# Moving a DMA broadcast from GpSimd's queue to the SP queue, with the stage orders chosen anew

## The chip, the core and the metric

The kernel runs on one core of a Trainium2 chip. The metric is the device time of one execution in microseconds (us). Engines are called as in the profile: PE (TensorE's matmuls), DVE (VectorE), ACT (ScalarE), POOL (GpSimd) and SP (SyncE, which here only issues DMAs).

## What is computed

The reference is a two-layer transformer block over 16 batch items of 256 tokens by 256 features, in float32. Cut to what matters here:

```python
xn = layernorm(x)                          # layer 0, per batch item
x  = x + attention0(xn) + gated_ffn(xn)    # 16 heads, hidden size 704
xn = layernorm(x)                          # layer 1
scores  = sigmoid(xn @ gate_w)             # 32 experts
combine = top-6 of scores, divided by their sum, zero elsewhere     # [token, expert]
g, u    = xn @ wg[e], xn @ wu[e]           # 96 hidden features for each expert e
routed  = sum over e of combine[:, e] * ((silu(g) * u) @ wd[e])
shared  = (silu(xn @ sg) * (xn @ su)) @ sd # 192 hidden features
x  = x + attention1(xn) + routed + shared
```

All 32 experts are computed for every token, and the routing weight multiplies the hidden activations.

## The kernel before

**Streams and bodies.** Batch items go through a software pipeline. One loop body (13 of them, iterations 2 to 14 of the 16 items; prologue and epilogue are written out with their own orders) works on four items at once, in five streams: stream 0 is layer 0 of one item (its queries `q0..q15`, the ffn chunks, the keys `k0..k15`), stream 1 is layer 1 of the item before (`o1`, `op`, `ln2`, `x`, `gram`, `k`, `rs+v`, `router`, `comb`, the stack loads, `Q0..Q14`, `MAX`, `K0..K14`, `T1`, `O`), streams 2 and 3 are the experts (stream 3 units 0 to 6 of that same item, stream 2 units 7 to 13 of the item before it), and stream 4 is the front of the next item (`f.ln`, `f.x`, `f.q`, `f.k`, `f.v`, `f.land`). These short names are used below and in the prediction.

**What sets the order.** Every engine runs the same list of stages, `ORDERS[...]`, a string of digits written out by hand: each digit names the stream whose next stage comes. Each engine is in order, so an instruction that waits for a semaphore holds everything behind it on that engine, and on SP a waiting DMA holds every later DMA.

**An expert unit** covers 256 hidden rows (two chunks of 128; units 0 and 1 are the shared expert and smaller). `gate` n: PE makes g in the bank s3r0 (12 matmuls), ACT takes tanh (L907), DVE makes `gs` (L1210), POOL multiplies it by the broadcast routing weights `cb2` (L704). `up` n: PE makes u in s3r1, DVE multiplies it by that product (L1205), ACT rounds it to half precision (L903), POOL makes the low part `h2l` (L713). `down` n: PE multiplies both by `wd` into s2acc (L1321).

**The routing weights.** Layer 1's router leaves [expert, token] weights in `comb_d` in DRAM (L511). `broadcast(group)` (L681 to L686) copies the weights of three units onto the 128 partitions of half of `cb2` with six DMAs, so four groups, 24 DMAs and 3 MB, for each item. Groups 0 and 1 are issued in stage `weights`, group 2 once POOL has finished the product of unit 4, and group 3 once it has finished that of unit 7, which frees their halves.

**The chain through SP.** When PE has made the values of the next item (`f.v`), ACT copies them to `v1`, and SP stores them (L458), loads the query and key rows (`land1`, 12 DMAs, L466), which DVE copies into `qst1` and `kst1` (L1027, stage `st`, needed by `q0`), then stores layer 0's attention output with 16 DMAs (L494), turns into the next body, and loads it back as `ot1` (L501, printed as xn<-o_d), which PE turns in stage `o1` (L1330, printed as s2r<-ident,xn).

Of the kernel before, what the change touches and what calls it, by code (L numbers as in the profile page):

```python
# [65 lines left out]
def prev(it):  # L66

    if isinstance(it, int):
# [12 lines left out]
    "body": ("022002102112020100102102212122210220210020121101212211131003201023100101011011310030004031"  # L81
             "40300040303043003433030330341333301"),
    "start": ("102003121002200012202302110030001030000221333131033100130000110020014121042110210033401132"
             "02341100012021310032304243131223121"),
    "first": ("010011220102012200010131011202030003020013211031201111010011321102112211310000400310422320"
             "32020240320043004013303103342323303"),
    "late": ("402220012014022102104101022121222102220120010021210121211413120301003102101331013311013303"
             "00140000330030034030000010303033133"),
    "end": ("220402100214201220121120121202400212200201222012140111011013312202113110313000030103011033"
             "03104030330143003000000133010303303"),  # L90
# [3 lines left out]
def program(nc, a, out):  # L94
# [22 lines left out]
    with ctx:  # L117
# [11 lines left out]
        def sem(name):  # L129
            if name not in sems:  # L130
                sems[name] = ctx.enter_context(nc.semaphore(name))
            return sems[name]
# [97 lines left out]
        cb2 = sb("cb2", [P, PAIRS, S])  # L230
# [303 lines left out]
        def sp3(sp, it, part):  # L534
            for kind, n in part:
                if (kind, n) == ("gate", 0):
                    sp.wait_ge(*emptied2(it, U2["x"]))
                    if prev(it) is not None:
                        sp.wait_ge(*event("ring3_full1", it, 0))
                    sp.dma_start(xe[:, :, :, :].rearrange("p g k s -> p (g k s)"),  # L540
                                 part2[:, 0:2, :, :].rearrange("p g k s -> p (g k s)")).then_inc(sem("xe_loaded"), 16)
                if kind == "out":
                    sp.wait_ge(*event("acc2_free", it, 1))
                    carry(sp, "sp_waited")
                    sp.dma_start(one(out, it).rearrange("b (t p) e -> p (b t) e", p=P), xbe[:, :, :]).then_inc(sem("out_saved"), 16)
                if (kind, n) != part[-1]:
                    yield
# [130 lines left out]
        def gp3(gp, it, part):  # L678
            g = nc.gpsimd

            def broadcast(group):  # L681
                src = one(comb_d, it).rearrange("b (a f) s -> f (b a) s", f=4)
                for i, first, count, which in ((0, 0, 3, 0), (0, 3, 1, 1), (1, 0, 2, 1), (1, 2, 2, 2), (2, 0, 1, 2), (2, 1, 3, 3)):
                    dst = cb2[32 * first:32 * (first + count), 6 * (group % 2):6 * (group % 2) + 6, :].rearrange("p (a i) s -> p a i s", i=3)[:, :, i, :]
                    gp.dma_start(dst, src[which, 2 * group:2 * group + 2].partition_broadcast(32 * count)  # L685
                                 ).then_inc(sem(f"cb2_loaded{group % 2}"), 16)  # L686

            for kind, n in part:
# [4 lines left out]
                if kind == "weights":  # L693
                    gp.wait_ge(*event("gc2_made", it, 0))
                    gp.wait_ge(*event("comb_saved", it, 16))
                    carry(gp, "gp_waited")
                    broadcast(0)
                    broadcast(1)
                if kind == "gate" and n >= 2:
# [6 lines left out]
                    if p in (2, 5):  # L706
                        gp.wait_ge(*event("gc2_made", it, p + 1))
                        broadcast(p // 3 + 2)
# [1019 lines left out]
```

## Time and profile before

| | |
|---|---|
| median of three runs | 2131.82 us (2128.59 to 2132.87) |
| the profiled execution, its own time | 2133.93 us |
| its span, first to last instruction | 2132.2 us |
| mean granted clock of PE | 0.968 of full speed |
| instructions | 48392 |
| period of the loop body, mean of twelve between two stores of the output | 124.4 us (1820.82 - 328.36 over 12) |

The profiled execution lies within 0.1% of the median, and its span is 1.7 us shorter than its own time. The first 268 us are set-up and prologue, the loop ends near 1885 us, and the last 80 us hold one item's rest, mostly its expert units alone.

### The profile page before, as it was taken

The numbers are of one execution on the slowest core, as the hardware profiler recorded it, in microseconds if no ns is written. First come the engines' busy times: TensorE is split into PE (matmuls) and PEld (weight loads), VectorE is DVE, ScalarE is ACT, GpSimd is POOL, SyncE is SP. The second block draws the span as 40 slices with busy tenths as digits, with TensorE's granted clock in tenths as the row PEclk, the third lists the DMA queues.
The fourth block names the chain that finished last, engine by engine and source line by source line (L and its number), as shares of the span: only waits on it lengthen the run. The fifth ranks groups of instructions, "written<-read, shape, count | busy, mean of one in ns | idle before, by whom it ended". The sixth has DMA issues, their size and how long they took to land.

```text
span 2132.2 us, 48392 instructions
## 1 busy us (share of the span) xinstructions
PE 1774.9 (83%) x16112; PEld 1340.1 (63%) x16112; DVE 1117.8 (52%) x2564; ACT 828.9 (39%) x1598; POOL 855.4 (40%) x988
## 2 busy tenths in 40 slices
PE   2747888889888888988888888888889888888887
PEld 1424666757666675766667576675757667676766
DVE  3566373655637365563636556373655637365442
ACT  2352425343343534334253433535343343533432
POOL 2003343534344353434435343443535344354445
PEclk7678999999999999999999999999999999999999
DMA  5452322313132132313213131321313132232111
GB/s 114 93 146 63 56 54 59 74 49 81 39 85 54 58 67 58 78 39 85 54 57 74 51 80 39 85 55 52 73 52 84 39 85 55 58 70 56 47 60 35
DMA packets 323775, 139.28 MB, mean 65 GB/s; under 512 B 228048, under 2 KB 309008, under 8 KB 323600
## 3 DMA queue, kind: packets, MB, share of 16 engines
q1 hardware_dynamic: 305168, 86.24, 17.9%
q0 software_dynamic: 18432, 50.36, 8.8%
q8 instruction: 153, 2.51, 0.5%
q14 instruction: 22, 0.18, 0.0%
HBM read 102.12 MB, written 29.88 MB: 62 GB/s over the span
## 4 chain that ended last, share of the span: by engine, by line
issue 33%; PE 28%; POOL 11%; DVE 11%; ACT 7%; SPq 6%; DMA 3%; POOLq 0%; ACTq 0%; DVEq 0%
PE s3r L1324 8%; POOL gs L704 4%; PE s2acc L1321 4%; POOL h2l L713 3%; SPq L494 2%; POOL cb L685 2%; PE s2r L1324 2%; SPq L519 2%; PE s1acc L1427 1%; ACT p L872 1%; PE s2r L1532 1%; ACT p L812 1%; DVE th L1205 1%; PE s2r L1575 1%; PE s1a L1324 1%
## 5 line engine op out<-in xcount | busy, mean ns | idle before, releaser
L704 POOL TENSOR_TENSOR gs<-gs,cb 128x512 f32<-128x512 f32 x192 | 243.8, 1270 | 403.0 <-DVE gs L1210 401.6
L713 POOL TENSOR_TENSOR h2l<-th,h2h 128x512 f16<-128x512 f32 (+1 forms) x224 | 247.1, 1103 | 355.6 <-ACT h2h L903 353.3
L903 ACT CAST h2h<-th 128x512 f16<-128x512 f32 (+1 forms) x224 | 131.7, 588 | 538.0 <-DVE th L1205 485.2
L1324 PE MATMUL s3r<-xe,xg 128*128 128x256 f16 x2304 | 285.7, 274 | 20.8 <-issue 20.8
L1321 PE MATMUL s2acc<-xd,h2h 128*128 128x256 f16 x1536 | 270.4, 278 | 19.3 <-POOL h2l L713 19.3
L1324 PE MATMUL s3r<-xe,xu 128*128 128x256 f16 x2304 | 283.3, 273 | 0.2 <-DVE th L1205 0.2
L1210 DVE SCALAR_TENSOR_TENSOR gs<-th,s3r 128x512 f32<-128x512 f32 (+1 forms) x224 | 144.9, 647 | 240.2 <-ACT th L907 240.0
L1324 PEld LDWEIGHTS s3r<-xe,xg 128*128 128x128 f16 x2304 | 223.9, 98 | 54.6 <-issue 25.0
L685 POOL DMA_DIRECT2D cb<-comb_d x384 | 229.6, 604 | 35.9 <-POOL gs L704 20.1
L1324 PEld LDWEIGHTS s3r<-xe,xu 128*128 128x128 f16 x2304 | 225.3, 98 | 27.3 <-DVE th L1205 0.5
L907 ACT ACTIVATE th<-s3r 128x512 f32<-128x512 f32 (+1 forms) x224 | 126.5, 565 | 274.0 <-PE s3r L1324 270.5
L1205 DVE TENSOR_TENSOR th<-s3r,gs 128x512 f32<-128x512 f32 x192 | 132.5, 690 | 164.4 <-POOL gs L704 152.8
L1321 PE MATMUL s2acc<-xd,h2l 128*128 128x256 f16 x768 | 213.6, 278 | 0.0
L1321 PEld LDWEIGHTS s2acc<-xd,h2h 128*128 128x128 f16 x1536 | 149.5, 99 | 50.4 <-POOL h2l L713 25.3
L650 POOL TENSOR_TENSOR h1p<-th,h1p 128x256 f16<-128x256 f32 x96 | 64.5, 671 | 235.2 <-ACT h1p L800 166.0
L1160 DVE TENSOR_REDUCE m<-s2r 128x3 f32<-128x384 f32 x256 | 131.0, 552 | 38.2 <-PE s2r L1534 33.3
L872 ACT ACTIVATE p<-s2r 128x384 f32<-128x384 f32 x256 | 111.1, 485 | 59.1 <-PE s2r L1578 59.1
L1532 PE MATMUL s2r<-stacks 126*128 126x128 f16 (+1 forms) x512 | 85.8, 256 | 45.5 <-DMA stacks<-part_d 28.7
L1038 DVE TENSOR_REDUCE mx<-s1a 128x2 f32<-128x512 f32 x128 | 87.6, 684 | 17.5 <-PE s1a L1403 16.3
L1532 PEld LDWEIGHTS s2r<-stacks 126*128 126x128 f16 x512 | 38.9, 100 | 90.1 <-DVE m L1160 51.0
L1038 DVE TENSOR_REDUCE mx<-s1b 128x2 f32<-128x512 f32 x128 | 87.5, 684 | 10.6 <-PE s1b L1403 10.5
L1575 PE MATMUL s2r<-stacks 128*128 128x256 f16 (+1 forms) x512 | 73.9, 249 | 19.2 <-DMA stacks<-mt 6.1
(279 smaller groups left out, 3125.9 us busy)
## 6 DMA issues: line engine op xcount, KB each, us to landing
cb<-comb_d POOLq DMA_DIRECT2D x128, 192.0 KB, 3.4
part_d<-part SPq DMA_DIRECT2D x32, 512.0 KB, 3.2
cb<-comb_d POOLq DMA_DIRECT2D x128, 128.0 KB, 3.1
stacks<-part_d SPq DMA_DIRECT2D x192, 64.0 KB, 2.3
va<-v_d SPq DMA_DIRECT2D x512, 8.0 KB
cb<-comb_d POOLq DMA_DIRECT2D x128, 64.0 KB, 3.1
land<-part_d SPq DMA_DIRECT2D x96, 64.0 KB, 2.5
part<-part_d SPq DMA_DIRECT2D x96, 64.0 KB, 4.2
```

The lines of the kernel that those rows point to most:

```text
L685: gp.dma_start(dst, src[which, 2 * group:2 * group + 2].partition_broadcast(32 * count)).then_inc(sem(f"cb2_loaded{group % 2}"), 16)
L704: g.tensor_tensor(gc2[:, p % 2, :], gs2[:, p % 2, :], cb2[:, 2 * (p % 6):2 * (p % 6) + 2, :].rearrange("p a s -> p (a s)"), ALU.mult).then ...
L713: g.tensor_tensor(h2l[0:m, n % 2, 0:w], th2[0:m, n % 2, 0:w], h2h[0:m, n % 2, 0:w], ALU.subtract).then_inc(sem("h2l_made"), 1)
L872: s.activation(p2[:, i % PSLOT, :], ring2[u % 2][:, 0:3 * P], ACT.Exp, scale=L ** -0.5).then_inc(empties2(u), 1)
L903: s.copy(h2h[0:m, n % 2, 0:w], th2[0:m, n % 2, 0:w]).then_inc(sem("h2h_made"), 1)
L1038: v.tensor_reduce(mx1[:, h, :], two(bk), AX.X, ALU.max).then_inc(empties1(u), 1)
L1160: v.tensor_reduce(m32[:, h, :], bk[:, 0:3 * P].rearrange("p (c n) -> p c n", n=P), AX.X, ALU.max).then_inc(empties2(u), 1)
L1205: ins = v.tensor_tensor(th2[0:m, s, 0:w], bk[0:m, 0:w], gc2[0:m, s, 0:w], ALU.mult)
L1210: v.scalar_tensor_tensor(gs2[0:m, s, 0:w], th2[0:m, s, 0:w], 1.0, ring3[0][0:m, 0:w], ALU.add, ALU.mult).then_inc(empties3(0), 1)
L1321: ins = nc.tensor.matmul(bk, lhs[i][k], rhs[j][k], start=first and chain[0], stop=last and chain[1], skip_group_check=True)
L1324: ins = nc.tensor.matmul(bk, lhs[i][k], rhs[j][k], start=first, stop=last)
L1532: mm(bk[:, P * j:P * j + P * (j + 1)], query(qst2, h, OPEN)[:, P * j:P * j + P], key(kst2, h, OPEN)[:, 0:P * (j + 1)], start=j == 0, stop= ...
```

## The change

The six-DMA helper `broadcast` moves from the GpSimd program `gp3` to the SP program `sp3`, with the same sources, destinations and semaphores. Groups 2 and 3 were issued by POOL behind its own product of unit 4 and 7, in the stages `gate4` and `gate7`; SP now waits for the semaphore of that product (`gc2_made`) in the same stages. All five order strings are replaced, for every engine.

```diff
 ORDERS = {
-    "body": ("022002102112020100102102212122210220210020121101212211131003201023100101011011310030004031"
-             "40300040303043003433030330341333301"),
+    "body": ("222020210011002210101220121022210212022200121002121111103123031321003100130101301101000401"
+             "03401300040304330030033040343301333"),
...
         def sp3(sp, it, part):
+            def broadcast(group):
+                src = one(comb_d, it).rearrange("b (a f) s -> f (b a) s", f=4)
+                for i, first, count, which in ((0, 0, 3, 0), (0, 3, 1, 1), (1, 0, 2, 1), (1, 2, 2, 2), (2, 0, 1, 2), (2, 1, 3, 3)):
+                    dst = cb2[32 * first:32 * (first + count), 6 * (group % 2):6 * (group % 2) + 6, :].rearrange("p (a i) s -> p a i s", i=3)[:, :, i, :]
+                    sp.dma_start(dst, src[which, 2 * group:2 * group + 2].partition_broadcast(32 * count)
+                                 ).then_inc(sem(f"cb2_loaded{group % 2}"), 16)
...
+                if kind == "weights":
+                    sp.wait_ge(*event("gc2_made", it, 0))
+                    carry(sp, "sp_waited")
+                    sp.wait_ge(*event("comb_saved", it, 16))
+                    broadcast(0)
+                    broadcast(1)
+                if kind == "gate" and n in (4, 7):
+                    sp.wait_ge(*event("gc2_made", it, n - 1))
+                    broadcast((n - 4) // 3 + 2)
...
         def gp3(gp, it, part):
...
-                if kind == "weights":
-                    gp.wait_ge(*event("gc2_made", it, 0))
-                    gp.wait_ge(*event("comb_saved", it, 16))
-                    carry(gp, "gp_waited")
-                    broadcast(0)
-                    broadcast(1)
...
-                    if p in (2, 5):
-                        gp.wait_ge(*event("gc2_made", it, p + 1))
-                        broadcast(p // 3 + 2)
```

Read as stages, the end of one body and the start of the next, up to `o1`, hold these after `f.v`. Before: down2 gate4 k15 up4 weigh3 down3 gate5 turned1 up5 f.land O down4 gate6 up6 down5 outproj, then st gate7 up7 q0 q1 down6 o1. Now: turned1 gate5 f.land up5 down4 outproj gate6 up6 down5, then gate7 up7 down6 st gate8 q0 up8 o1.

On the SP queue the start of the loop body stood like this before (`va` are the loads of layer 0's values, `xn<-o_d` the load for `o1`):

```order
L477 DMA va<-v_d 8x16x16
L477 ISA
L477 DMA va<-v_d 8x16x16
L477 ISA
L477 DMA va<-v_d 8x16x16
L477 ISA
L477 DMA va<-v_d 8x16x16
L497 REGISTER_ALU
L500 ISA
L501 ISA
L501 DMA xn<-o_d 128x2x256
```

and now:

```order
L539 DMA cb<-comb_d 96x2x256
L539 ISA
L539 DMA cb<-comb_d 32x2x256
L539 DMA cb<-comb_d 64x2x256
...
L477 DMA va<-v_d 8x16x16
L477 ISA
L477 DMA va<-v_d 8x16x16
L497 REGISTER_ALU
L500 ISA
L501 ISA
L501 DMA xn<-o_d 128x2x256
```

Six broadcasts of group 3 (three of them in the rows left out) now stand ahead of the load for `o1`, and two value loads in place of four.

On DVE the start of the loop body before:

```order
L1306 ISA
L1027 COPY qst<-land 48x8x64 x4
L1027 COPY kst<-part 48x8x64 x4
L1208 ISA
L1209 ISA
L1210 SCALAR_TENSOR_TENSOR gs<-th,s3r 128x512
L1204 REGISTER_ALU
L1205 TENSOR_TENSOR th<-s3r,gs 128x512
L1036 ISA
L1038 TENSOR_REDUCE mx<-s1a 128x2
```

and now:

```order
L1306 ISA
L1209 ISA
L1210 SCALAR_TENSOR_TENSOR gs<-th,s3r 128x512
L1204 REGISTER_ALU
L1205 TENSOR_TENSOR th<-s3r,gs 128x512
L1021 ISA
L1027 COPY qst<-land 48x8x64 x4
L1027 COPY kst<-part 48x8x64 x4
L1208 REGISTER_ALU
L1209 REGISTER_ALU
L1210 SCALAR_TENSOR_TENSOR gs<-th,s3r 128x512
L1036 ISA
```

The copies into `qst` and `kst` now stand behind both halves of unit 7 and ahead of unit 8's `gs`.

On ACT the tanh of unit 9 (L907) now stands between the square root of `ln2` (L762) and that of the key norm (L842). Before:

```order
L762 ACT_TABLE_LOAD
L762 ACTIVATE mv<-mv 128x2
L902 REGISTER_ALU
L903 CAST h2h<-th 128x512
L839 CAST part<-s2r 128x512
L842 ACTIVATE rt<-rt 128x32
```

and now:

```order
L762 ACT_TABLE_LOAD
L762 ACTIVATE mv<-mv 128x2
L907 ACT_TABLE_LOAD
L907 ACTIVATE th<-s3r 128x512
...
L839 CAST part<-s2r 128x512
L842 ACT_TABLE_LOAD
L842 ACTIVATE rt<-rt 128x32
```

The body has six table loads on ACT now, where it had four.

## Rows read from the trace of the kernel before

**Rows 1.** the page: busy share of each engine, with instructions.

```profile
PE 1774.9 (83%) x16112; PEld 1340.1 (63%) x16112; DVE 1117.8 (52%) x2564; ACT 828.9 (39%) x1598; POOL 855.4 (40%) x988
```

**Rows 2.** windows of one body: us; busy PE, PEld, DVE, ACT, POOL; clock, DMA share, GB/s.

```profile
369.66:393.76 24.10, 21.64 (x203) 18.34 (x201) 10.43 (x23) 6.71 (x12) 13.47 (x14) 1.00 0.55 103
393.76:431.67 37.91, 31.70 (x297) 26.40 (x296) 28.26 (x65) 14.51 (x28) 19.36 (x22) 1.00 0.23 60
431.67:492.92 61.25, 53.74 (x507) 37.40 (x508) 28.09 (x69) 28.35 (x57) 19.95 (x25) 1.00 0.16 50
```

**Rows 3.** TensorE's waits in twelve bodies (total us, times, longest).

```profile
PE s2r L1532 <- DMA stacks<-part_d: 24.7, 12, 2.4
PE s2r L1522 <- DVE cm L1152: 23.0, 12, 1.9
PE s3r L1324 <- issue: 20.8, 12, 2.1
...
PE s2acc L1321 <- POOL h2l L713: 9.5, 12, 2.1
...
PE s2r L1330 <- DMA xn<-o_d: 6.4, 7, 2.1
```

**Rows 4.** timeline of the SP queue around the end of a body.

```profile
370.99 0.38 SPq L458 DMA_DIRECT2D v_d<-xn  x1
371.69 2.90 SPq L466 DMA_DIRECT2D land<-part_d  x6
374.77 3.68 SPq L466 DMA_DIRECT2D part<-part_d  x6
379.99 7.70 SPq L494 DMA_DIRECT2D o_d<-th  x16
388.46 1.70 SPq L477 DMA_DIRECT2D va<-v_d  x4
390.61 0.39 SPq L501 DMA_DIRECT2D xn<-o_d  x1
```

**Rows 5.** timeline of TensorE in the same stretch.

```profile
369.44 0.38 PE L1324 MATMUL s1b<-wqkv,x1l 128*128 128x256 f16 x2
...
393.76 0.60 PE L1330 MATMUL s2r<-ident,xn 128*128 128x128 f32 x4
```

**Rows 6.** timeline of all engines, unit 4 from gate matmuls to up product.

```profile
370.96 1.47 PE L1324 MATMUL s3r<-xe,xg 128*128 128x256 f16 x12
...
372.27 0.38 PE L1444 MATMUL s1a<-qst,kst 128*128 128x256 f16 x2
...
372.60 1.47 PE L1324 MATMUL s3r<-xe,xu 128*128 128x256 f16 x12
...
373.87 1.28 POOL L704 TENSOR_TENSOR gs<-gs,cb 128x512 f32<-128x512 f32 x1 [2.28 <-DVE gs L1210]
...
374.00 1.06 PE L1427 MATMUL s1acc<-p,va 128*17 128x256 f32 x16
...
375.18 0.69 DVE L1205 TENSOR_TENSOR th<-s3r,gs 128x512 f32<-128x512 f32 x1 [1.39 <-POOL gs L704]
```

**Rows 7.** instructions by source line: ns min/median/max, first and last start.

```profile
L477 SPq DMA_DIRECT2D va<-v_d x512: 275/278/2792, 51.7 to 1944.9; - x171
...
L558 SPq DMA_DIRECT2D sd_row<-in_L_ffn_s_down x1: 588/588/588, 28.5 to 28.5; - x1
...
L1027 DVE COPY kst<-part x64: 410/420/426, 54.4 to 1885.8; 48x512 f32<-48x512 f32 x64
```

**Rows 8.** timeline of GpSimd, then of TensorE, in the last 80 us.

```profile
2096.59 2.37 POOL L685 DMA_DIRECT2D cb<-comb_d  x4 [1.09 <-issue]
...
2100.20 0.61 PE L1321 MATMUL s2acc<-xd,h2h 128*128 128x256 f16 x2 [3.37 <-POOL h2l L713]
```

**Rows 9.** timeline of ScalarE around the second layer's square roots.

```profile
407.10 1.28 ACT L845 ACT_TABLE_LOAD   x1
408.40 0.22 ACT L845 ACTIVATE el<-s2r 128x64 f32<-128x64 f32 x1
```

More of the change, by code:

```diff
@@ L80 @@
 ORDERS = {
-    "body": ("022002102112020100102102212122210220210020121101212211131003201023100101011011310030004031"
-             "40300040303043003433030330341333301"),
[L83 to L90, printed above, removed]
+    "body": ("222020210011002210101220121022210212022200121002121111103123031321003100130101301101000401"
+             "03401300040304330030033040343301333"),
+    "start": ("103112303000102300212023203012121030330020300101002100130002033000431211310342001112020413"
+             "10022400303100021321111122130114422"),
+    "first": ("001002110011001031101132223000021101021021312302300021210100112111131120001003023243104302"
+             "30301420030304000244230022323310332"),
+    "late": ("220202102410102021002110221012221021220202112121211101310030310221003103031014013110100033"
+             "03400330401003030000434103030333013"),
+    "end": ("022402040240002200201021212011102112021201022202100110112000124410021031002020331100330131"
+             "30013313040000101331331333330133010"),
 }
@@ L679, in gp3 @@
             g = nc.gpsimd
[L681 to L686, printed above, removed]
             for kind, n in part:
```

## The prediction

> **What bounds the kernel now.** The page comes first: PE is busy for 83% of the span, no other engine for more than 52%, POOL for 40% [rows 1]. The page's slices are alike from the eighth on, since the loop runs 13 like bodies, so I cut one body by windows at three joints of PE's order: from the end of `f.v` to `o1` (24.10 us, PE busy 21.64), from `o1` to `Q0` (37.91, busy 31.70), and from `Q0` to the end of the next `f.v` (61.25, busy 53.74) [rows 2]. Together 123.26 us with 107.08 busy: 16.2 us of PE's idleness is all that a new order can win or add to in a body. The chain of waits says who holds PE there. In twelve bodies the layer 1 chain leads: 24.7 us for the stack loads, 23.0 for the router's `cm`, 20.8 for the turn of the loop (`issue`), against 9.5 for POOL's `h2l` and 6.4 for the load that `o1` needs [rows 3]. So POOL, which the change relieves, holds PE for 0.8 us in a body, and SP's chain, which the change loads, for 0.5 us, on average: it is covered, but only just.
>
> That chain is the one to read closely. `f.v` ends on PE at 369.66 (its last two matmuls start at 369.44 and take 0.11 each to the next start) [rows 5]. SP stores the values at 370.99, loads 12 row sets from 371.69, stores layer 0's output with 16 DMAs from 379.99, turns into the next body, loads four value sets, and issues the load for `o1` at 390.61 [rows 4]. PE starts `o1` at 393.76 [rows 5], and no wait is put down there in this body, so 3.15 us was enough for the load to land. SP is nearly without pause from 371.69 to 390.61. PE's own work in that stretch is as long as SP's chain, and that is why neither waits.
>
> **The change part by part.**
>
> *POOL's issues go.* Where they held PE, that stops. In the loop they do so inside the stretch from `f.v` to `o1`, whose length another chain sets below, so I count nothing for it there. In the last 80 us the experts run alone, and the broadcast of group 3 (its last four DMAs take 2.37 us) precedes the `h2l` for which PE waits 3.37 us; PE then runs slower, a pair of matmuls takes 0.61 us [rows 8] where such a pair takes 0.38 [rows 5], as at the lower clock level. I take 3.4 us, 1.7 us for the lower clock (an estimate: half of a stretch as long as the gap), and 0.5 us of shorter waits: 5.6 us gained. Bounds: 3 and 9 us.
>
> *Less PE work covers SP's chain.* Count the stages that the change section lists. Gone from between `f.v` and `o1` are down2, gate4, up4 and down3 (1.31 us each, as gate4 from 370.96 to 372.27), k15 and q1 (0.33 each, 372.27 to 372.60), weigh3 (1.0, from 374.00) [rows 6] and O (0.4, four transposes like those of `o1`); new are gate8 and up8. Net -5.24 - 2.06 + 2.62 = -4.7 us. So PE has 21.64 - 4.7 = 16.9 us to do there, and 107.08 - 16.9 = 90.1 us in the rest of the body.
>
> *The chain itself is no shorter.* From `f.v` to the store 1.33 us, from there to the load for `o1` 19.62 us, from there to `o1` 3.15 us. Off: the gap ahead of the output stores (378.45 to 379.99, of which 0.2 us is ordinary), since `turned1` is now directly behind `f.v` and the stores come later than its result: -1.3; two value loads fewer, of four in 1.70 us with their register instructions: -0.96. On: six broadcasts of group 3. No such DMA from SP is in the trace. Its bounds: a value load's 0.28 us of issue plus 0.1 us around it, and the only partition broadcast timed, `sd_row` at 0.59 plus 0.07 [rows 7]: six take 2.3 to 4.0 us. I take 0.46 us each, near the bulk of SP's DMAs, 2.75 us. The six are free to go: POOL's product of unit 7 comes first. Sum: 24.10 - 1.3 - 0.96 + 2.75 = 24.6 us, bounds 24.1 to 25.9, against 16.9 us of work and 1.7 us for the turn of the loop (20.8 us in twelve [rows 3]). PE waits some 6 us more than nothing here, where it waited 0.5.
>
> Broadcast group 2 stands between the stores of `part_d` and of the values. PE has up3, down2, k12 with its weighing, k13 and gate4 (5.6 us) and then k14, k15, up4, down3, weigh3 and f.v (5.6 us) after `f.k`; POOL's product of unit 4 ends 2.9 us behind its gate matmuls (372.27 to 375.15 [rows 6]), so SP is through about 1 us before the values are there. Hidden; if it is not, each us late is added.
>
> *A second chain in the same place.* DVE's copies for `q0` stand behind unit 7 now. From the end of gate7's matmuls to the end of the up product is 3.6 us (372.27 to 375.8 [rows 6]), eight copies follow, at 0.38 us apart (0.42 each, overlapping) 3.1 us [rows 7]. PE has up7, down6 and gate8 to cover that, 3.9 us: `q0` waits 2.7 us. Were SP's chain instant, `o1` would come 20.9 us after `f.v`. This wait lies under the longer chain and costs nothing more, but it is the floor.
>
> *The rest of the body.* From `o1` on, the same links with other cover, each by its before-wait and by what moved: `op` has lost gate8 as cover, +0.8; `x` to `gram` +1.1; `rs` -0.4; the router's `cm` has ffn0 as new cover, -1.1; the stack loads the same (down11 is new cover, but ACT's copy `ct` stands behind a later tanh); five pairs Q6 to Q14 in a row, which DVE reduces at 1.0 us a pair, +0.6; the K pairs are spaced better, -0.9; `f.x` +0.4. Sum +0.5, bounds -5 and +4, since eight guesses of half a microsecond each can lean one way. In `x` to `gram` 0.7 us comes from ACT: the tanh of unit 9 between two square roots makes two more table loads in a body. One takes 1.28 us here and the activation starts 0.02 us behind it (407.10, 408.40) [rows 9]. The Trainium skill (ScalarE: Activation LUTs, What ACT_TABLE_LOAD costs) adds a drain of about 1.38 us to each switch of tables. By that the body would be up to 1.4 us longer; the trace shows no such drain, so I leave it out.
>
> *Sum.* Body: 24.6 + 90.1 + 13.7 (idle in the two other stretches, 6.21 + 7.51) + 0.5 = 128.9 us against 123.3, +5.6 us. Twelve joints of body to body: +67 us. The last 80 us: -5.6 us. The prologue's and epilogue's orders I count at 0, +-8. Against the profiled execution's own 2133.9 us this gives 2195; that execution is 2 us above the median, so 2193 us.
>
> **The rivals.**
>
> *Refilled cover, faster (0.15).* The work that left the stretch (4.7 us) could be worth more elsewhere: if it falls just into the waits for `cm`, for the stacks and for the K pairs (1.9 + 2.0 + some 3 us a body), the idleness in the rest drops from 13.7 to 7 us. The body is then 24.6 + 90.1 + 7 = 121.7 us, -1.6, so 2131.8 - 19 - 5.6 = 2107 us. It decides from 9.0 us of idleness downwards. For it: nothing but those waits is large. Against: stack loads, `cm` and K pairs keep nearly the cover they had, as counted.
>
> *Half refilled (0.20).* With 11 us of idleness there: 125.7, +2.4, 2155 us; in its lower tail lies no change (0.04).
>
> *Transfers queue on SP's queue, worse (0.15).* The load for `o1` is now issued 1 us behind six broadcasts that write 768 KB; if it lands only behind them, 2 to 3 us later, the body is +8.6 and the time 2229 us. Against: the queue's DMAs finished in about 3 us at the joint even with 16 output stores ahead.
>
> *The issuer does not matter, no change.* The Trainium skill (DMA: Bandwidth & Descriptors, Issuing engines are not separate DMA queues) says that DMAs of all issuers share the same 16 DMA engines, and that another issuer saves only its issue time, usually small. By that, moving them is worth 24 issues a body on either side and the time would be about 2130 us, within the 0.04. The trace agrees that bytes are not the limit (DMA share 0.55 at most [rows 2]), but here issue time lies on a chain, so I give it no more.
>
> **How the numbers follow.** The forecast, 2165 to 2215, has 0.46; with worse 0.15 and the half refilled case's slower part 0.20 this is 0.81 for slower by over 0.2% (what this measurement can tell from no change), 0.04 for the same, 0.15 for faster. The range 2120 to 2240 us leaves out most of the faster rival and the tail of the worse one. The predicted time is the likeliest case's, 2193 us; its own range is 2165 to 2215.
>
> **What would show it.** PE's wait for the load of `o1` rises from 6.4 us in all to 25 us or more, with a wait for the copies into `kst` or `qst` of 2 to 3 us ahead of `q0` in each body, new in the list of waits. From `f.v` to `o1` stays near 24.6 us while PE is busy for about 17 of them; the period of the bodies rises from 124.4 to about 129 us. On SP, six broadcasts at the body's start take 2.3 to 4 us. POOL has 384 instructions fewer, and PE's wait of 3.4 us for `h2l` in the last 80 us is gone. I am wrong if the idleness from `o1` to the next `f.v` falls below 9 us.

## The result: 4.65% slower, and the profile after

The changed kernel takes 2230.35 us (median; 2227.28 to 2235.62), the kernel before 2132.35 us beside it: a ratio of 1.0465, 95% interval 1.0437 to 1.0492. The profiled execution of the changed kernel has a span of 2225.6 us.

The page, busy share of each engine (answers to [rows 1]):

```profile
PE 1819.6 (82%) x16112; PEld 1362.2 (61%) x16112; DVE 1105.2 (50%) x2564; ACT 866.1 (39%) x1624; POOL 625.2 (28%) x604
```

POOL is relieved of 384 instructions and 230 us, and nothing is faster for it. PE, with the same 16112 matmuls, is busy 45 us longer: a part of it ran at a lower granted clock.

Windows of one body, cut at the same three joints as [rows 2]: from the end of `f.v` to `o1`, to `Q0`, to the end of the next `f.v`:

```profile
645.07:672.30 27.23, 18.21 (x152) 15.05 (x150) 10.97 (x22) 5.09 (x9) 9.90 (x8) 0.94 0.47 108
672.30:710.15 37.85, 32.80 (x286) 26.59 (x285) 24.41 (x60) 15.67 (x27) 12.67 (x13) 0.91 0.15 39
710.15:776.97 66.82, 60.13 (x572) 42.23 (x570) 30.62 (x73) 31.77 (x64) 15.73 (x16) 1.00 0.17 51
```

The first window holds 152 matmuls in place of 203 and is 3.1 us longer; PE is idle in it for 9.0 us, where it was idle for 2.5. In the two others it is idle for 11.7 us, where it was for 13.7. The clock is 0.94 and 0.91 in the first two; it was 1.00 in all three.

PE's waits between 300 and 1900 us, which hold twelve bodies (answers to [rows 3]; total us, times, longest):

```profile
PE s2r L1330 <- DMA xn<-o_d: 43.8, 12, 6.3
PE s1a L1401 <- DVE kst L1027: 38.5, 12, 3.7
PE s3r L1324 <- issue: 25.9, 12, 2.6
...
PE s2r L1532 <- DMA stacks<-part_d: 15.1, 13, 1.4
...
PE s2r L1522 <- DVE cm L1152: 8.8, 13, 0.7
```

The load for `o1`, next to nothing before (6.4), leads, and the copies into `kst` are new. The waits for the stacks and `cm` have shrunk by 24 us together.

Timeline of SP's queue around the same joint (answers to [rows 4]):

```profile
641.96 4.09 SPq L539 DMA_DIRECT2D cb<-comb_d  x6
646.28 0.42 SPq L458 DMA_DIRECT2D v_d<-xn  x1
647.01 2.92 SPq L466 DMA_DIRECT2D land<-part_d  x6
650.11 3.10 SPq L466 DMA_DIRECT2D part<-part_d  x6
653.40 6.60 SPq L494 DMA_DIRECT2D o_d<-th  x16
663.22 3.70 SPq L539 DMA_DIRECT2D cb<-comb_d  x6
667.61 0.75 SPq L477 DMA_DIRECT2D va<-v_d  x2
668.81 0.40 SPq L501 DMA_DIRECT2D xn<-o_d  x1
```

The six broadcasts before the load take 3.70 us. Ahead of them is a hole: the last store is issued at 660.00, the first broadcast at 663.22, and nothing is waited for. That is SP's turn of the loop. It took 0.29 us before and takes 2.5 to 2.8 us in each of the twelve turns now.

Timelines of PE, then of DVE, there (answer to [rows 5]):

```profile
644.40 0.38 PE L1324 MATMUL s1b<-wqkv,x1l 128*128 128x256 f16 x2
...
665.74 0.39 PE L1401 MATMUL s1a<-kst,qst 126*128 126x256 f16 x2 [3.67 <-DVE kst L1027]
...
671.97 0.65 PE L1330 MATMUL s2r<-ident,xn 128*128 128x128 f32 x4 [3.08 <-DMA xn<-o_d]
```

```profile
660.96 0.69 DVE L1205 TENSOR_TENSOR th<-s3r,gs 128x512 f32<-128x512 f32 x1 [1.37 <-POOL gs L707]
661.57 2.48 DVE L1027 COPY qst<-land 48x512 f32<-48x512 f32 x4
664.08 1.53 DVE L1027 COPY kst<-part 48x512 f32<-48x512 f32 x4
```

Two windows of the same eleven bodies, of before and then of after, say what the longer body is made of (columns as in [rows 2]):

```profile
385.40:1754.80 1369.40, 1187.95 (x11025) 907.51 (x11023) 735.09 (x1705) 546.16 (x1067) 580.20 (x661) 0.99 0.26 63
```

```profile
387.60:1838.80 1451.20, 1226.08 (x11025) 925.01 (x11023) 725.85 (x1706) 577.86 (x1089) 421.39 (x396) 0.95 0.23 60
```

81.8 us more in eleven bodies, 7.4 each: 38.1 of PE's busy time for the same 11025 matmuls, and 43.7 of idleness. The whole span by its parts (up to the first turn of the loop, twelve bodies, the rest): 385, 1495 and 251 us before, 387, 1582 and 256 us now, cut where PE turns. All but 6 us of the loss is in the loop.

The chain from `f.v` to `o1`, step by step, read off SP's and PE's records, in us (medians over eleven joints, so a row's steps add up only nearly to its total). "v_d" is the store of the values, "land" the first row load, "o_d" the first store of layer 0's output, "turn" the time from the branch at the end of SP's loop to its next instruction, and "load" the issue of the load for `o1`. The last five rows are experiments told below:

```
                       f.v to  v_d to  land to  o_d to  turn  broad-  to the  load to  total
                       v_d     land    o_d      turn          casts   load    o1
before                 1.22    0.69    8.31     8.41    0.29  -       2.46    3.07     24.7
changed                1.61    0.73    6.45     6.74    2.62  3.97    1.91    3.14     27.2
broadcasts on SP,
  old orders           1.22    8.62    6.28     6.91    2.68  4.00    2.84    2.91     35.5
group 3 behind load    1.67    0.73    6.42     6.77    2.66  -       1.71    3.15     23.7
group 3 late, st first 1.88    0.73    6.44     6.86    2.60  -       1.68    2.98     23.2
head on SP, new orders 0.82    0.70    6.09     6.59    0.30  -       1.54    5.67     22.3
SP's loop of 493       1.22    0.70    8.31     8.22    2.75  -       2.64    3.26     27.1
```

### The profile page after: what moved, and what is told of

The parts are those of the page before. It is cut to its first block, busy times and chain, and to the rows that moved or that the text cites. A ratio compares the mean times of both kernels' runs of the same rounds, so it can differ in the third digit from the quotient of the medians.

```text
span 2225.6 us, 48390 instructions
## 1 busy us (share of the span) xinstructions
PE 1819.6 (82%) x16112; PEld 1362.2 (61%) x16112; DVE 1105.2 (50%) x2564; ACT 866.1 (39%) x1624; POOL 625.2 (28%) x604
## 4 chain that ended last, share of the span: by engine, by line
issue 64%; POOL 18%; PE 6%; DVE 3%; ACT 2%; SPq 1%; DMA 1%; POOLq 1%; DVEq 0%; ACTq 0%
POOL gs L707 8%; POOL h2l L713 7%; PE s3r L1324 2%; POOL h1p L666 1%; PE s2acc L1321 1%; POOL gs L679 1%; POOL va L689 1%; DVE th L1205 1%; SPq L539 0%; DMA xn<-o_d 0%; ACT h2h L903 0%; PE s1acc L1427 0%; ACT p L872 0%; PE s2r L1575 0%; ACT p L812 0%
## 5 line engine op out<-in xcount | busy, mean ns | idle before, releaser
L1324 PE MATMUL s3r<-xe,xg 128*128 128x256 f16 x2304 | 289.2, 276 | 25.9 <-issue 25.9
L1324 PE MATMUL s3r<-xe,xu 128*128 128x256 f16 x2304 | 303.4, 285 | 0.0
L1321 PE MATMUL s2acc<-xd,h2h 128*128 128x256 f16 x1536 | 263.3, 273 | 3.4 <-POOL h2l L713 3.1
L1324 PEld LDWEIGHTS s3r<-xe,xu 128*128 128x128 f16 x2304 | 235.2, 102 | 36.6 <-issue 0.6
L907 ACT ACTIVATE th<-s3r 128x512 f32<-128x512 f32 (+1 forms) x224 | 126.6, 565 | 244.4 <-PE s3r L1324 242.0
L1401 PE MATMUL s1a<-kst,qst 126*128 126x256 f16 x256 | 56.2, 306 | 65.2 <-DVE kst L1027 63.5
L800 ACT CAST h1p<-th 128x256 f16<-128x256 f32 x96 | 38.8, 405 | 158.1 <-DVE th L1074 158.1
L812 ACT ACTIVATE p<-s1b 128x512 f32<-128x512 f32 x128 | 76.8, 600 | 52.3 <-PE s1b L1446 37.0
L701 POOL TENSOR_TENSOR xbe<-x,bo_row 128x512 f32<-128x512 f32 x16 | 20.3, 1266 | 257.2 <-DMA out<-xbe 198.2
```

The costliest lines, as they stand in the source:

```text
L907: s.activation(th2[0:m, n % 2, 0:w], ring3[0][0:m, 0:w], ACT.Tanh, scale=0.5).then_inc(sem("th2_made"), 1)
L1321: ins = nc.tensor.matmul(bk, lhs[i][k], rhs[j][k], start=first and chain[0], stop=last and chain[1], skip_group_check=True)
L1324: ins = nc.tensor.matmul(bk, lhs[i][k], rhs[j][k], start=first, stop=last)
```

## The experiments

Ratios are to the kernel before, with 95% intervals.

**Orders and issuer, each alone.** First the new orders with all broadcasts left on POOL:

```diff
 ORDERS = {
-    "body": ("022002102112020100102102212122210220210020121101212211131003201023100101011011310030004031"
+    "body": ("222020210011002210101220121022210212022200121002121111103123031321003100130101301101000401"
...
```

> The new orders with the broadcasts left on POOL: SP's code is that of before, POOL's too. Theory A (the queue move itself costs the time: six broadcasts of 4.2 us and a turn of SP's loop of 2.65 in place of 0.29 us, both on the chain from f.v to o1): the chain shrinks from 27.8 us to 27.8 - 4.2 - 2.4 = 21.2 us, close to the floor that the copies for q0 set (20.9 to 22), and the body from 131.9 to about 125.5 us, so the time is near 2150 us; SP's turn is 0.3 us again. Rival B (the new orders cost it, by moving 4.7 us of PE work away from this chain): the time stays at 2190 us or above. Rival C (POOL's issues cost as much where they were): 2200 us or above, with POOL's products late and new waits of PE for h2l.

It took 2303.19 us, 1.0749 (1.0709 to 1.0790): worse than the changed kernel, and far from the 2150 us of theory A. The waits of PE, and POOL's timeline at the place:

```profile
PE s1acc L1384 <- POOL h1p L650: 91.5, 24, 9.4
PE s1a L1401 <- DVE kst L1027: 31.1, 11, 3.1
```

```profile
478.02 4.73 POOL L685 DMA_DIRECT2D cb<-comb_d  x8
485.61 2.43 POOL L685 DMA_DIRECT2D cb<-comb_d  x4 [2.86 <-issue]
488.05 1.30 POOL L650 TENSOR_TENSOR h1p<-th,h1p 128x256 f16<-128x256 f32 x2
```

Groups 0 and 1 stand in the new order ahead of layer 0's `ffn3` and `ffn4`; on POOL their twelve issues take 10 us, and PE waits 7.6 us a body for `h1p` behind them. SP's chain did get short (22.8 us), which helps nothing. So each order suits one issuer.

Then the broadcasts on SP with the orders of before:

> The broadcasts on SP with the orders of before. Group 3 then falls behind unit 7's gate, which in the old order is ahead of o1, and groups 0 to 2 ahead of the stores of f.k and f.v. Theory A (the move itself costs): SP's chain from f.v to o1 is 24.1 + 4.2 (six broadcasts) + 2.4 (turn of the loop) = 30.7 us or above against 24.1 before, all of it uncovered: +6.6 us a body and a time of 2132 + 12 x 6.6 = 2211 us or above, with a wait for the load of o1 of some 6 us a body. Rival B (the orders cost): 2150 us or less, and this version is faster than the changed kernel by over 3%. If A holds and the new orders were a repair, the time is above the changed kernel's 2230 us.

2301.93 us, 1.0761 (1.0734 to 1.0788). The sign and the place are theory A's; the size is not. SP's timeline:

```profile
523.89 4.07 SPq L539 DMA_DIRECT2D cb<-comb_d  x6
528.27 2.82 SPq L466 DMA_DIRECT2D land<-part_d  x6
531.27 3.10 SPq L466 DMA_DIRECT2D part<-part_d  x6
534.55 8.41 SPq L494 DMA_DIRECT2D o_d<-th  x16
546.00 3.65 SPq L539 DMA_DIRECT2D cb<-comb_d  x6
```

I had left group 2 out: in the old order it stands behind `v_d`, so it and its wait for POOL's product of unit 4 are on the chain too (8.62 us from `v_d` to the loads in place of 0.69). PE waits 121.9 us for the load of `o1` in eleven bodies. The new orders are thus a repair of what the move to SP costs (7.6% down to 4.65%); they don't reach what POOL with its own orders had.

**Group 3 behind the load for `o1`.**

```diff
-                if kind == "gate" and n in (4, 7):
-                    sp.wait_ge(*event("gc2_made", it, n - 1))
-                    broadcast((n - 4) // 3 + 2)
+                if kind == "gate" and n == 4:
+                    sp.wait_ge(*event("gc2_made", it, 3))
+                    broadcast(2)
+                if kind == "down" and n == 7:
+                    sp.wait_ge(*event("gc2_made", it, 6))
+                    broadcast(3)
```

> The changed kernel with one thing moved: SP issues broadcast group 3 behind down7 instead of behind gate7, so after the load for o1. Theory A: the load for o1 is issued 4.2 us earlier, PE's wait for it (3.65 us a body, 43.8 in twelve) falls to nearly nothing, and f.v to o1 goes from 27.8 to about 24 us, where the copies for q0 (3.2 us a body) hold next; the body gets 3 to 3.7 us shorter, so the time is 2186 to 2195 us. The rival in which the load waits for the bytes of the broadcasts on the queue gives the same sign but more, 4.2 + 1 us a body, 2170 us. The rival in which the second chain (copies behind unit 7, 3.2 us a body) already holds PE: less than 1 us a body, above 2218 us. A late group 3 would show as waits of POOL for cb2 and of PE for h2l of units 8 and 9.

2176.38 us, 1.0170 (1.0141 to 1.0198): the loss falls from 4.65 to 1.70%, the profiled span from 2225.6 to 2177.2 us. This is theory A's mechanism, and a larger gain than its 2186 to 2195 us. The step "broadcasts" goes from 3.97 us to none and no other step changes. The window of eleven bodies (388.5 us on):

```profile
388.50:1791.10 1402.60, 1204.15 (x11024) 914.94 (x11022) 726.05 (x1706) 576.91 (x1089) 422.02 (x396) 0.98 0.24 62
```

Of the 48.6 us won in them against the changed kernel's eleven, 22 are PE's busy time at equal work: the stretches at the half clock (1.2 GHz) add up to 65 us in place of 137. That is why more is won than the wait removed.

**The stack stage first**, so that DVE's copies for `q0` no longer stand behind unit 7 (one digit):

```diff
-    "body": ("222020210011...
+    "body": ("022220210011...
```

> The changed kernel with one digit moved: the stage that copies the stacks for q0 runs at the body's start, ahead of gate7, up7 and down6, so DVE's copies no longer stand behind unit 7. Theory A (from f.v to o1 one chain counts, SP's, with the load for o1 at its end; the wait for the copies lies under it): PE's wait of 38.5 us in all for kst is gone, the wait for the load of o1 rises from 43.8 us by most of it, f.v to o1 stays at 27.8 us and the time at 2225 to 2235 us. Rival (the second chain holds PE by itself and sets what follows): each body is 1 to 3 us shorter, 2195 to 2218 us.

2235.54 us, 1.0461 (1.0441 to 1.0481), at the upper end of what theory A had: the wait for `kst` is gone, and the one for the load, 43.8 us in the changed kernel, has grown by more than its 38.5 us.

```profile
PE s2r L1330 <- DMA xn<-o_d: 94.7, 12, 10.4
```

With both changes together:

> Both single changes together: group 3 behind the load for o1, and the stage with the copies for q0 first. In the first alone f.v to o1 is 23.9 us on average, with 3.2 us a body of waiting for kst and 0.4 for the load. Theory A: with the copies early only SP's chain is left, which ends (load for o1 issued at 529.05, 3 us to land) at nearly the same time, so f.v to o1 gets 0 to 1 us shorter and the time is 2165 to 2178 us. Rival (the copies set it): f.v to o1 falls to 21 us and the time to 2145 us or less. What is left above 2138 us is then in the rest of the body and in the clock.

2172.74 us, 1.0160 (1.0141 to 1.0180); `f.v` to `o1` is 23.2 us (23.7 with group 3 moved alone), and PE now waits 38.1 us for the load in twelve bodies in place of 4.7. The two chains end nearly together, so removing one gives nothing. The window of its eleven bodies says what the remaining 1.6% are made of:

```profile
387.50:1790.10 1402.60, 1217.54 (x11024) 923.11 (x11023) 725.59 (x1705) 578.36 (x1089) 421.43 (x396) 0.96 0.24 62
```

It is 33.2 us longer than before's. PE is idle in it for 185.1 us, where it was for 181.5, and busy for 1217.5 in place of 1188.0: nearly all of it is work at the half clock (99 us of such stretches in place of 20). So it is not the amount of idleness alone that lowers the clock. What in these orders does it was not tested.

**What the turn of SP's loop costs, and why.** To the kernel before, semaphore increments are added in a stretch in which SP is idle: 70 in the first kernel, 250 in the second.

```diff
             sp.dma_start(x1[:, :, :], one(a["L0_attn_x"], it)...
+            for n in range(70):
+                carry(sp, "sp_waited")
```

> The kernel before with 70 semaphore increments more in SP's loop, in a stretch in which SP is idle, so that its loop is as long as the changed kernel's (310 instructions in place of 243); no DMA and no wait is added. Theory A2 (SP's loop, once long enough, is fetched anew at each turn, and this is what the 2.65 us are): the turn takes 2.3 us or more instead of 0.29, SP's queue for instructions shows some 80 packets in place of 22, the load for o1 comes 2.4 us later, and as PE waits for it by 0.5 us already the body gets 1.9 to 2.4 us longer: 2155 to 2161 us. Rival A3 (the turn is long since SP has many DMAs in flight when it branches, or since the next broadcasts are slow to issue): the turn stays at 0.3 us and the time at 2132 us.

> The kernel before with 250 semaphore increments in SP's loop (493 instructions a turn, no DMA more) in a stretch in which SP is idle for 20 us. With 70 (313 instructions) the turn stayed at 0.25 us, where the changed kernel with 310 instructions, 108 of them DMAs against 84, takes 2.6 us. Theory A4 (what counts is the size of the loop's code, and a DMA takes several times the room of an increment): the turn takes 2.3 us or more, the queue of instructions shows some 100 packets in place of 24, and the time is about 2160 us. Rival A5 (what counts is the DMAs themselves): the turn stays at 0.3 us and the time at 2138 us.

With 70 the time is 2141.32 us, 1.0019 (1.0005 to 1.0034), and the turn 0.25 us: theory A2 as I had put it fell, since the number of instructions alone (313 here, 310 in the changed kernel) does not decide. With 250 it is 2189.95 us, 1.0242 (1.0216 to 1.0269; from two executions only), and the turn 2.5 to 3.2 us. The queue of instructions, in the changed kernel, with 70, with 250, and in the kernel with the head on SP (below):

```profile
q14 instruction: 82, 0.67, 0.1%
```

```profile
q14 instruction: 24, 0.20, 0.0%
```

```profile
q14 instruction: 102, 0.84, 0.1%
```

```profile
q14 instruction: 22, 0.18, 0.0%
```

So a loop of SP that is long enough is loaded again at each turn, and that without any DMA more. The times of these packets settle it: the kernel before has none between 361 and 1900 us; the changed kernel has exactly 5 in every body, the kernel with 250 has 6, and in each of their twelve long turns one starts 0.9 to 1.2 us behind the branch, inside the hole. Four loops bound its size: 276 instructions with 96 DMAs (0.30 us) and 313 with 84 (0.25 us) turn quickly, 310 with 108 and 493 with 84 slowly. These fit together if a DMA takes more room than an increment: at three times the room they are 468, 481, 526 and 661 units, an estimate from the counts alone. The factor three is my choice; any above 1.13 puts the four in this order. At 8.2 KB a packet (0.67 MB in 82) the two long loops fetch 41 and 49 KB a turn. The Trainium skill (Advanced Engine Details and Errata, ISA Cache) gives 32 KB for an engine other than TensorE, loaded in lines of 256 instructions, so 512 of them; the trace agrees with such a limit between 481 and 526 units, but shows no sizes of instructions.

The slow turn holds PE also without any broadcast on SP: in the kernel with 250 increments the chain is 2.4 us longer, and twelve bodies take 1533 us in place of 1495, 3.15 us each. A further 22 us lie ahead of the loop, where the same increments are issued too; they are no part of the turn's price.

**Only groups 0 and 1 on SP**, where it is idle, groups 2 and 3 on POOL; first with the orders of before:

```diff
+        def sp3(sp, it, part):
+                if kind == "weights":
+                    sp.wait_ge(*event("gc2_made", it, 0))
+                    carry(sp, "sp_waited")
+                    sp.wait_ge(*event("comb_saved", it, 16))
+                    broadcast(0)
+                    broadcast(1)
...
         def gp3(gp, it, part):
-                if kind == "weights":
...
-                    broadcast(0)
-                    broadcast(1)
```

> The orders of before, broadcast groups 0 and 1 on SP (12 DMAs a body, in a stretch of some 12 us in which SP is idle) and groups 2 and 3 on POOL as before, so none stands on the chain from f.v to o1. Theory A (an issue costs time only where it stands on that chain): no loss, and a gain of what POOL's issues held PE for, at most 0.9 us a body: 2124 to 2138 us, if SP's turn of the loop stays at 0.3 us; if the turn becomes 2.6 us with 12 more DMAs in the loop, its 2.3 us stand on the chain and the time is 2158 to 2168 us. Rival (the queue does not matter, wherever it stands): 2138 us in either case.

2135.12 us, 0.9993 (0.9978 to 1.0008), the turn 0.30 us: as theory A says, twelve broadcasts a body on SP cost nothing off the chain. The rival, by which the queue never matters, had the same time here; it is the kernel with all four groups on SP (7.6%) that rules it out. The hoped-for gain from POOL's relief isn't there.

Then the same with the new orders:

> The changed kernel's orders, groups 0 and 1 on SP, groups 2 and 3 on POOL. SP's loop is then 276 instructions with 96 DMAs, for which the turn was 0.3 us. Theory A (the changed kernel's loss is what stands on SP's chain): against group 3 moved behind the load (2176 us, 127.5 us a body) the turn's 2.3 us and group 2's 1 us of delay are gone too, the wait for the copies of q0 (3.2 us a body) sets f.v to o1 at 21 to 22 us, and the body is 1.5 to 3 us shorter: 2140 to 2160 us. Rival (the new orders are good once SP's chain is relieved): the body falls below 124.4 us and the time below 2130 us. Rival (POOL's issues of groups 2 and 3 hold PE under these orders, as those of groups 0 and 1 did): waits of PE for h2l or h1p of 1 us a body and more, above 2165 us.

2175.94 us, 1.0196 (1.0178 to 1.0214). This missed all three: the time is in the third's range, but its sign is not there (PE waits 8.4 us for `h1p` in thirteen waits, as in the changed kernel, and 1.0 us for `h2l`). SP's chain is relieved of the turn and of group 2's delay (the load is issued 16.2 us behind `f.v`, with group 3 moved it was 20.0), and the time is that of the kernel with group 3 moved. PE's waits there:

```profile
PE s1a L1408 <- DVE kst L1034: 33.0, 12, 3.0
...
PE s2r L1331 <- DVE part L1089: 24.3, 12, 2.9
```

The load for `o1` is in time; PE reaches `o1` late, held by the copies for `q0` (2.8 us a body), and behind `o1` it waits for DVE's `part` (2.0 us a body, line 1082 in the changed kernel, where it is 0.3). The body is 127.1 us. So 2.5 us a body of the loss, and 9 us behind the loop (261 us in place of 251), are there with SP's chain relieved; I put them down to the new orders themselves. More than half of it is again PE's busy time: 1203.3 us in place of 1188.0 in the eleven bodies, with 61 us at the half clock, and 219.3 in place of 212.9 behind the loop. A kernel with both reliefs at once, this one with the copies for `q0` first, was not run.

**Is the lower clock a cost of the waits?** Matmuls whose results nothing reads are put ahead of PE's two long waits: 24 of 128 columns in each, then 14 of 512 columns.

```diff
+        def idle(bk, count):
+            for n in range(count):
+                nc.tensor.matmul(bk[:, :], ident16[:, :], xg[0][:, 0, 0:512], start=True, stop=True, skip_group_check=True)
...
             yield
+            if not isinstance(it, int):
+                pe.wait_ge(*free1(it, U1["q_rows", 0]))
+                idle(ring1[U1["q_rows", 0] % 2], 14)
             pe.wait_ge(*event("stack1_made", it, 2))
...
+            if isinstance(it, Before):
+                pe.wait_ge(*free2(it, U2["o1"]))
+                idle(ring2[U2["o1"] % 2], 14)
             pe.wait_ge(*event("ot1_loaded", it, 16))
```

> The changed kernel with 24 matmuls more, whose results nothing reads, ahead of each of PE's two long waits at a body's start (for kst, 3.2 us, and for the load of o1, 3.65 us, on average). Each takes 0.107 us at the full clock, 24 of them 2.6 us, so they fit into the waits, and the chains of SP and DVE are as long as before. Theory C (half of the loss in the loop, 38 of 82 us in eleven bodies, is PE's lower granted clock, which follows these waits): the stretches at the half clock (136 us in the loop) nearly go, the joints stay 27.8 us, and the time falls by 20 to 40 us, to 2190 to 2210 us. Rival (the lower clock has another cause, or only moves waiting into work): half clock as before and 2225 to 2245 us, the upper end where the fillers run at the half clock and end later than the load.

> As the kernel with 24 small matmuls in each of the two waits, but with 14 larger ones (512 columns in place of 128) in each; the 24 took 1.50 us, by which estimate 14 of four times the columns take some 3 us or more, as long as the waits of 3.2 and 3.65 us. In that run 2.3 and 5.0 us of waiting were left, the half clock fell only from 136 to 119 us in the loop, and SP's chain from f.v to o1 was 1.1 us longer. Theory C (PE's lower clock comes of these waits): the half clock in the loop falls below 60 us and PE's busy time without the added matmuls by 25 us or more from 1226 us in eleven bodies; the time falls below 2225 us unless the chain gets longer again. Rival (it does not come of them): 110 to 140 us at the half clock, and 2235 us or more.

The first took 2237.82 us, 1.0470 (1.0449 to 1.0490), in the rival's range and not in theory C's, but it decides little: I had mis-sized it (24 took 1.50 us, not 2.6), long waits were left, and SP's chain got 1.1 us longer. The trace shows where: the row loads, whose step is 8.0 us in place of 6.45, have one or two single issues of 1.0 to 1.9 us in most bodies, each with a packet of instructions on queue 8 within 0.5 us of its start (more of this below). The second took 2213.65 us, 1.0362 (1.0338 to 1.0387), 1.0% less than the changed kernel although PE does more. Timeline of PE in one joint, and the window of eleven bodies:

```profile
659.88 3.18 PE L1338 MATMUL s1a<-xg,ident 128*128 128x512 f16 x14
...
665.30 3.19 PE L1338 MATMUL s2r<-xg,ident 128*128 128x512 f16 x14
...
669.74 0.66 PE L1330 MATMUL s2r<-ident,xn 128*128 128x128 f32 x4 [1.26 <-DMA xn<-o_d]
```

```profile
387.90:1825.80 1437.90, 1266.68 (x11333) 944.12 (x11331) 726.46 (x1706) 578.49 (x1089) 422.11 (x396) 0.98 0.24 60
```

308 added matmuls at 3.18 us for 14 are 70 us; without them PE is busy for 1197 us in place of 1226. Stretches at the half clock in the eleven bodies add up to 55 us, where the changed kernel has 137 and the one before 20. Both bounds of theory C hold: filling these two waits takes away most of the lower clock, though 34 us more of it are left than the kernel before has. `f.v` to `o1` is hardly shorter (26.8 us in place of 27.2), so most of the gain lies behind it.

**POOL relieved in the last pass only.** As the kernel with groups 0 and 1 on SP and the orders of before, but in the last pass groups 2 and 3 are SP's too:

```diff
+                if isinstance(it, int) and it == B - 1 and kind == "gate" and n in (4, 7):
+                    sp.wait_ge(*event("gc2_made", it, n - 1))
+                    broadcast((n - 4) // 3 + 2)
```

> The orders of before, groups 0 and 1 on SP, groups 2 and 3 on POOL, but in the last pass (in which no chain of layer 0 or 1 is left that SP could delay) groups 2 and 3 on SP too. Theory A and the prediction's first term: PE's wait of 3.4 us for h2l in the last 80 us is gone, and 3 to 5.6 us with it, so 2130 to 2134 us against 2138 us of before, and SP's turn of the loop stays at 0.3 us. Rival (the wait is put to h2l, but is set by the broadcast's landing, 3 us behind its issue, not by POOL's time for issuing it): 0 to 1 us, 2135 to 2138 us.

2129.50 us, 0.9979 (0.9965 to 0.9993), the only version whose interval lies below the kernel before. PE's wait for `h2l` in the last 88 us:

```profile
PE s2acc L1334 <- POOL h2l L726: 3.0, 3, 2.6
```

It was 7.1 us in six waits, 3.4 the longest, and 5.9 in six with POOL issuing in the last pass; what follows the loop takes 248.7 us where it took 252.5 with the same loop and POOL issuing. Those 3.8 us are one execution against one, and the same two executions differ by 4.5 us ahead of the loop, where their code is the same; the intervals of the two ratios overlap. So the shorter wait is shown, and a gain of about 3 us from it is likely, not shown. This small part is all that the idea gives.

## Why the prediction was right, point by point

The sign, the mechanism (SP's chain from `f.v` to `o1`, made longer with less work of PE to cover it) and the wide range held. The time came out 37 us above 2193 and outside the likeliest case's own 2165 to 2215: terms of the sum were mis-sized and two were missing. In the profiled executions the loop is 87 us longer, where 67 were forecast, and what follows it 4.5 us longer, where 5.6 less were forecast.

- **"POOL's issues go", 5.6 us gained in the last 80 us.** Over-sized. The longest wait for `h2l` there fell only from 3.4 to 2.7 us in the changed kernel and is not gone, and the part of the run behind the loop is 4.5 us longer, not shorter. With the old orders and the last pass on SP it is 3.8 us between two executions, which is no more than such executions differ by.
- **"Less PE work covers SP's chain", 16.9 us of work.** Measured 18.2 at a clock of 0.94, with 152 matmuls in place of 203. Right, but for the clock.
- **"The chain itself is no shorter", 24.6 us, bounds 24.1 to 25.9.** Measured 27.2 (mean 27.8), outside. Of its terms: six broadcasts 3.97 in place of 2.75 (my upper bound, from the one `sd_row`, was right, and I took a value in the lower half); the stores and the gap ahead of them shorter by more than the 1.3 taken (8.31 and 8.41 to 6.45 and 6.74, so -3.5); and **missing**: SP's turn of the loop, +2.3, which I had carried over unchanged. Without it the chain would have been 24.9. The joint that I started from, 24.10, was also a short one: the median before is 24.7.
- **Why the row loads and stores got shorter by more.** Two single issues at fixed places of the chain are slow before, and the traces say beside what. The fifth of the 16 output stores takes 1.1 to 2.2 us in all twelve bodies, with POOL's group 2 issued 1.5 to 6.3 us ahead of it; with the same orders and the broadcasts on SP it takes 0.31 to 0.32 us in all twelve, and the step 6.91 in place of 8.41 us. One of the row loads takes 1.3 to 1.7 us in eleven of twelve bodies, and in each of the eleven a packet of instructions on queue 8 starts up to 0.3 us ahead of it; in the twelfth body the nearest starts 0.3 us behind its start, and it takes 0.32 us. This second cause is a coincidence in time that no run tests. DMA traffic of the kernel before (packets, MB, share of 16 engines) between 505.0 and 506.0 us, at such a store, then between 498.0 and 500.5 us, at such a row load:

```profile
q0 software_dynamic: 37, 0.12, 76.7%
```

```profile
q8 instruction: 1, 0.02, 3.7%
```

- **"Hidden" for group 2.** Not quite: the store of the values is issued 1.61 us behind `f.v`, and 0.82 where group 2 isn't on SP, so some 0.8 us are on the chain.
- **"A second chain", 2.7 us for `q0`, nothing more.** 3.2 us (copies 4.0 in place of 3.1), and under SP's chain as said: taking it away left the time as it was. The second half, a floor of 20.9 us, was optimistic: with SP's chain relieved `o1` came at 22.3.
- **"The rest of the body", +0.5, 104.3 us in all.** Measured 104.7, right by two errors that cancel. Idleness there fell by 2.0 us (11.7 in place of 13.7; 14.2 was predicted), as the half refilled rival said, through the shorter waits for `cm` and the stacks. Against it PE's busy time there is 92.9 us in place of 90.1, by the clock.
- **No term for the clock.** This was the largest omission: 38 us of PE's busy time in eleven bodies, 3.5 each. With two waits of 3 us close together at each body's start PE runs at 1.2 GHz in parts of the next 20 us.
- **The rivals.** "Transfers queue on SP's queue" gave 2229 us, the measured number, by a mechanism that is not there: from the load's issue to `o1` it is 3.14 us behind broadcasts and 3.07 before. That the number fits is luck. "The issuer does not matter", on the Trainium skill (DMA: Bandwidth & Descriptors, Issuing engines are not separate DMA queues), which calls the issue time usually small: with the orders held the same, the issuer alone moves the time from 1.000 to 1.076 of the kernel before, or from 1.075 to 1.0465. About the transfers the traces agree: the broadcasts land 2.9 us behind their issue from SP and 3.2 from POOL (medians). What counts here is where the issues stand on a chain.
- **No drain at a table switch.** The stretch `x` to `gram`, with the two more table loads in a body, is 2.5 us where it was 2.6 (medians of all bodies). The new load ahead of unit 9's tanh starts at 679.31 and takes 1.28 us, and the tanh starts at 680.60. So ScalarE's switches added nothing like 1.4 us. PE's wait for `part` (L1096) in this stretch did rise from 3.8 to 16.4 us in twelve bodies, the +1.1 of the forecast, but only because less of PE's work lies there now.

The loss, by the runs: of 4.65% group 3 ahead of the load is 2.95 (changed kernel against the one that moves it; 45% of it by the clock). The other 1.70% is, as far as these runs tell, the new orders' own: 2.5 us in each of twelve bodies and 9 us behind the loop, 39 us in all, which are there without group 2 on SP and without the long turn too. These two (0.8 and 2.3 us on SP's chain) are hidden as soon as group 3 is gone, since the copies for `q0` then hold PE; so the shares are not a sum of independent costs. Which stages of the new orders make those 39 us beyond the two waits named is not settled; more than half of them is PE's busy time at the lower clock.

## What to carry to other kernels

Moving issues to another queue is a change to the chains of both engines: price them at the place in which each will stand, with the engine's own turn of the loop, and look whether the loop's code grows past what turns quickly (the turn went from 0.29 to 2.6 us). Leave what the longest chain waits for ahead of what nobody waits for: one broadcast group behind the load gave back six tenths of the loss. And price a wait of some microseconds on TensorE at more than its length, since the work behind it may run at half the clock; here 4 us of idleness a body brought 3.5 us of slower work with it, and in the kernel with both single changes 0.3 us of it went with 2.7 us of slower work. So compare the granted clock of whole stretches too, and not only the waits.

## What the runs showed of the hardware that was not expected

- SP's loop is fetched anew at each turn once it is long enough: 0.25 to 0.30 us a turn for 243, 276 and 313 instructions, 2.5 to 3.2 us for 310 (108 of them DMAs) and 493, with 5 and 6 packets a turn on the queue of instructions where the short loops have none.
- In the changed kernel SP issues broadcasts over 32 to 96 partitions in 0.3 to 1.4 us each, 3.2 to 4.7 us for six, where most of its other DMAs take 0.28 to 0.43 us; POOL needs 2.4 us for four, the same rate. The issuer does not make them cheaper.
- Useless matmuls made the changed kernel faster: 28 more a body, 1.0% less time.
- POOL's broadcasts slow an issue of SP: the same store of the same orders takes 1.1 to 2.2 us with them shortly ahead and 0.31 us without. Of the 59 issues of SP over 0.9 us in the kernel before, 43 have a packet of instructions from 0.8 us ahead of their start to their end; of the 821 between 0.25 and 0.34 us it is 8%.
